# A gated delta-rule layer with a ternary feed-forward on one core: matrices and merge of the next pair placed ahead of the head scaling

## The reference, cut to what matters

```python
# x: [8, 256, 256] float32; 6 heads, DK = 32, DV = 64
q = silu(causal_conv4(x @ Wq.T)); k = silu(causal_conv4(x @ Wk.T)); v = silu(causal_conv4(x @ Wv.T))
beta = sigmoid(x @ Wb.T)
g = -exp(A_log) * softplus(x @ Wa.T + dt_bias)
q = l2norm(q) * DK ** -0.5; k = l2norm(k)
for t in range(T):                      # per batch row and head
    S = S * exp(g[t])
    S = S + beta[t] * outer(k[t], v[t] - k[t] @ S)
    o[t] = q[t] @ S
o = o * rsqrt(mean(o * o) + 1e-5) * norm_w * silu(x @ Wg.T)
h = layernorm(x + o @ Wo.T)
hq = where(h > 0.33, 0.5, where(h < -0.33, -0.5, 0))
wq = where(W > 0.2, 0.6, where(W < -0.2, -0.6, 0)) + rram_variation
return layernorm(h + hq @ wq.T)
```

## Time and profile before

| | |
|---|---|
| time, median of 3 runs | 342.59 us (339.65 to 344.24) |
| the profiled execution, its own time | 342.39 us |
| its span, and what lies around it | 340.6 us, 1.8 us |
| PE busy | 253.0 us (74%) |
| DVE busy | 260.6 us (77%) |
| ACT busy | 153.5 us (45%) |
| POOL busy | 9.2 us (3%) |
| mean DMA rate | 29 GB/s |

### The profile page before, as it was taken

How to read it: one execution, slowest core, us unless ns; L and a number is a source line. 1 busy time by engine, 2 the same in 40 slices (tenths; PEclk the granted TensorE clock), 3 DMA queues, 4 the chain that set the end, 5 groups by cost and what they waited for, 6 DMA issues and landing times.

```text
span 340.6 us, 15160 instructions
## 1 busy us (share of the span) xinstructions
PE 253.0 (74%) x6980; PEld 173.2 (51%) x6980; DVE 260.6 (77%) x648; ACT 153.5 (45%) x283; POOL 9.2 (3%) x14
## 2 busy tenths in 40 slices
PE   1969845799678977987689949988828449957561
PEld 0435412475565554756554635767607348755331
DVE  0588999774799996886999995979999951429966
ACT  1487773155664701736547405665423034235031
POOL 2110000000100000001000000010000000000000
PEclk9999987599989996999999967999987858999898
DMA  7900000000000001000000110000010002000101
GB/s 218 379 13 2 3 1 0 4 4 4 6 4 4 1 0 65 6 4 4 5 7 0 62 38 30 6 5 6 4 62 2 0 6 66 4 5 8 58 2 63
DMA packets 8032, 9.83 MB, mean 29 GB/s; under 512 B 1568, under 2 KB 7072, under 8 KB 7968
## 3 DMA queue, kind: packets, MB, share of 16 engines
q1 hardware_dynamic: 6480, 8.39, 7.3%
q10 hardware_dynamic: 1488, 0.47, 0.6%
HBM read 6.76 MB, written 2.10 MB: 26 GB/s over the span
## 4 chain that ended last, share of the span: by engine, by line
PE 54%; DVE 21%; issue 15%; ACT 7%; DMA 2%; DVEq 0%; SPq 0%; ACTq 0%
PE fr L322 15%; PE pj L335 10%; PE pj L350 5%; PE pg L322 5%; PE pc L322 4%; PE fr L425 4%; PE po L322 3%; PE pc L484 3%; DVE conv_buf L976 3%; PE po L484 2%; PE pj L514 2%; DMA xt<-x_t 2%; ACT kq L692 2%; DVE tok_buf L988 1%; DVE ss L1009 1%
## 5 line engine op out<-in xcount | busy, mean ns | idle before, releaser
L335 PE MATMUL pj<-xt,wproj 128*128 128x512 f32 x96 | 51.2, 682 | 8.9 <-DMA xt<-x_t 7.1
L976 DVE SCALAR_TENSOR_TENSOR conv_buf<-raw,wconv,conv_buf 128x512 f32<-128x512 f32 x72 | 53.4, 755 | 4.8 <-ACT conv_buf L668 3.1
L335 PEld LDWEIGHTS pj<-xt,wproj 128*128 128x128 f32 x96 | 19.4, 213 | 32.1 <-issue 25.0
L667 ACT ACTIVATE raw<-pj 128x512 f32<-128x512 f32 x24 | 14.3, 596 | 31.3 <-PE pj L335 31.3
L350 PE MATMUL pj<-xt,wproj 128*128 128x512 f32 x48 | 24.8, 659 | 4.5 <-ACT conv_buf L668 4.5
L322 PE MATMUL fr<-x_t,x 32*32 32x16 f32 x768 | 10.7, 204 | 20.7 <-issue 20.7
L322 PEld LDWEIGHTS fr<-x_t,x 32*32 32x32 f32 x768 | 10.1, 142 | 21.9 <-issue 21.9
L350 PEld LDWEIGHTS pj<-xt,wproj 128*128 128x128 f32 x48 | 10.0, 212 | 16.3 <-issue 8.4
L988 DVE STREAM_TRANSPOSE tok_buf<-kq 128x1536 f32<-128x1536 f32 x4 | 7.1, 1776 | 13.5 <-ACT kq L692 13.5
L732 ACT ACTIVATE mq<-fr 128x512 f32<-128x512 f32 x12 | 7.2, 597 | 22.1 <-PE fr L322 22.1
L322 PEld LDWEIGHTS fr<-kga,wu 32*32 32x32 f32 x768 | 11.4, 105 | 10.2 <-issue 10.2
(11 more groups left out here) (183 smaller groups left out, 569.0 us busy)
## 6 DMA issues: line engine op xcount, KB each, us to landing
xt<-x_t SPq DMA_DIRECT2D x1, 1536.0 KB, 11.9
res<-x SPq DMA_DIRECT2D x3, 512.0 KB, 4.1
out<-hid_buf SPq DMA_DIRECT2D x6, 256.0 KB, 2.1
wproj<-w_proj SPq DMA_DIRECT2D x1, 1024.0 KB, 8.0
xt<-x_t SPq DMA_DIRECT2D x1, 512.0 KB, 5.7
kq<-x SPq DMA_DIRECT2D x1, 512.0 KB, 3.9
wout<-w_out SPq DMA_DIRECT2D x1, 384.0 KB, 12.1
cst<-consts ACTq DMA_DIRECT2D x1, 305.5 KB, 11.1
```

What stands on the lines that cost most here:

```text
L335: mm = pe.matmul(pj[:, j % 2, :], wproj[:, t, j * P:(j + 1) * P], xt[:, t, k * TOK:(k + 1) * TOK], start=(t == 0), stop=(t == KT - 1))
L667: act.activation(raw[:, j, :, TAPS - 1:], bank, ACT.Copy)
L976: e = dve.scalar_tensor_tensor(out=conv[:, d, :, :], in0=raw[:, d, :, m:m + T], scalar=wconv[:, j, m:m + 1], in1=conv[:, d, :, :], op0=ALU ...
```

## The change

The order of the three lists is changed, and with it which PSUM banks some steps use.

- DVE: `head_norm` is split into `head_factors` (sum, rsqrt) and `head_scale` (scaling and transposes). `head_factors(k)` stays ahead of `chunk_matrices(k + 1)`; `head_scale(k)` and `gated(k)` stand behind `inverse_to_rows(k + 1)`, at the end of the turn. In the next turn `inverse` comes first, then two `conv_taps`, the attention sums and first norm of pair k - 1, two more `conv_taps`, `ternary`, `kq_to_tokens`, and the last two `conv_taps`.
- PE: `chunk_products` stand ahead of `exponents`. Behind the four projections of pair k + 2 come the gates of pair k (of both pairs 2 and 3 in turn 2), projections 4 and 5 of pair k + 2, then `merge(k + 1)`. `project_out(k - 1)` stands between `merge_second(k)` and `solved(k)` and writes to the banks of `pj`. `ternary_turned(k - 1)` moves behind chunk 2 of the loop, the two `feed_forward` parts behind chunks 3 and 4.
- ACT: `normalize(k - 1, 0)` moves behind `state_out(k, 0)`, `ternary_out` to chunk 3, the third `silu` ahead of the third transition's copy, the three value `silu` to chunks 4 to 6, all head squares behind the loop; the gates' SiLU and two tile copies close the turn.
- The ternary values move from `tok_buf` to `hid_buf`; the last pair's gate goes to used columns of `xt`.
- Last turn: the first half of the last heads (`end_heads(0)`) is done inside the turn behind `ternary`, the second half at its end.
- The prologue has no gates; projections 4 and 5 of pair 1 stand ahead of `merge(0)`.

```diff
--- before.py
+++ after.py
...
 gate = view(gate_buf, 0, GATE_TILES, TOK)
+gate_last = (xt[:, 0, 0:TOK], xt[:, 0, TOK:2 * TOK], xt[:, 1, 0:TOK])
...
 res = sb("res", [P, TT, HID])
-pos = view(tok_buf, 0, TT, HID, dt=BF16)
-xq = view(tok_buf, TT * HID // 2, TT, HID, dt=BF16)
+pos = view(hid_buf, 0, TT, HID, dt=BF16)
+xq = view(hid_buf, TT * HID // 2, TT, HID, dt=BF16)
...
 f_bank = (pj[:, 1, :], pj[:, 0, :])
+a_bank = (pj[:, 0, :], pj[:, 1, :])
+
+def gate_bank(k, j):
+
+    return pj[:, (j + (k == PAIRS - 1)) % 2, :]
...
             after(pe, tile_out, j - 1, k, CONV_TILES)
-        if not first(k) and j >= 4:
-            after(pe, gate_done, GATE_TILES, k - 1, GATE_TILES)
+        if k > 1 and j >= 4:
+            after(pe, gate_done, GATE_TILES, k - 2, GATE_TILES)
...
     def gates(k, j):
...
-        if j < 2:
-            if last(k):
-                after(pe, dexp_done, 1, k, 1)
-            else:
-                after(pe, tile_out, j + 3, k + 1, CONV_TILES)
+        if last(k):
+            gone = GATE_TILES * (k - 1) + j + 2
+            pe.wait_ge(gate_done, gone)
+        elif j == 2:
+            after(pe, gate_done, 1, k, GATE_TILES)
+        elif last(k + 1):
+            after(pe, dexp_done, 1, k + 1, 1)
         else:
-            after(pe, gate_done, 1, k, GATE_TILES)
+            after(pe, tile_out, j + 3, k + 2, CONV_TILES)
...
             w = CONV_TILES + j
-            mm = pe.matmul(pj[:, j % 2, :], wproj[:, t, w * P:(w + 1) * P],
+            mm = pe.matmul(gate_bank(k, j), wproj[:, t, w * P:(w + 1) * P],
...
         after(pe, tile_out, CONV_TILES, k, CONV_TILES)
-        if not first(k):
-            after(pe, gate_done, 0, k, GATE_TILES)
-            after(pe, ffn_in, 0, k - 1, 2)
+        if k > 1:
+            after(pe, ffn_in, 2, k - 2, 2)
...
             after(pe, v_tok_done, 1, k, 1)
-            if not first(k):
-                after(pe, y_in, 0, k, 2)
...
             after(pe, og_done, GATE_TILES, k, GATE_TILES)
+            if last(k + 1):
+                after(pe, gate_done, GATE_TILES, k + 1, GATE_TILES)
+            else:
+                after(pe, tile_out, CONV_TILES, k + 2, CONV_TILES)
...
             for j in range(GATE_TILES):
-                mm = pe.matmul(y_bank[part][:, (n % 2) * HID:(n % 2 + 1) * HID],
+                mm = pe.matmul(a_bank[part][:, (n % 2) * HID:(n % 2 + 1) * HID],
...
     def ternary_turned(k):
...
         after(pe, xq_done, 1, k, 1)
-        if last(k + 1):
-            after(pe, gate_done, GATE_TILES, k + 1, GATE_TILES)
-        else:
-            after(pe, tile_out, 5, k + 2, CONV_TILES)
...
                 pe.wait_ge(w_split, 3)
-            if not last(k + 1):
-                after(pe, tile_out, CONV_TILES, k + 2, CONV_TILES)
...
     def turn(k, front):
         merge_second(k)
-        if front:
-            project(k + 1, 5)
-        solved(k, 0)
-        solved(k, 1)
-        if not first(k):
-            ternary_turned(k - 1)
-        for b in range(2, 5):
+        if not first(k):
+            project_out(k - 1, 0)
+            project_out(k - 1, 1)
+        for b in range(5):
...
             transitions(k, b)
-            if not front and b < 2:
-                feed_forward(k - 1, b)
...
             heads_out(k, c)
-            if front and not first(k) and c in (2, 3):
-                feed_forward(k - 1, c - 2)
+            if not first(k) and c == 2:
+                ternary_turned(k - 1)
+            if not first(k) and c in (3, 4):
+                feed_forward(k - 1, c - 3)
         if front:
-            exponents(k + 1)
...
                 chunk_products(k + 1, g)
+            exponents(k + 1)
...
                     project(k + 2, j)
-            gates(k + 1, 0)
-            gates(k + 1, 1)
-            project_out(k, 0)
-            project_out(k, 1)
-            gates(k + 1, 2)
+            for j in range(GATE_TILES):
+                gates(k, j)
+            if last(k + 1):
+                for j in range(GATE_TILES):
+                    gates(k + 1, j)
+            else:
+                project(k + 2, 4)
+                project(k + 2, 5)
             merge(k + 1)
-            if not last(k + 1):
-                project(k + 2, 4)
...
     def decay_gate(i):
...
         project(1, j)
-    for j in range(GATE_TILES):
-        gates(0, j)
     decay_sums(1)
+    project(1, 4)
+    project(1, 5)
     merge(0)
-    project(1, 4)
...
     def gate_silu(k, j):
         after(act, gate_mm, j + 1, k, GATE_TILES)
-        if j == 0 and not first(k):
+        if j == 0 and not first(k) and not last(k):
             after(act, og_done, 0, k, GATE_TILES)
-        act.activation(gate[:, j, :], pj[:, j % 2, :], ACT.Silu).then_inc(gate_done, 1)
+        dst = gate_last[j] if last(k) else gate[:, j, :]
+        act.activation(dst, gate_bank(k, j), ACT.Silu).then_inc(gate_done, 1)
...
     def normalize(k, n):
...
             weight_part(1)
-        if front:
-            tile_out_of_psum(k + 1, 4)
-        if not first(k):
-            normalize(k - 1, 0)
-        if front:
-            tile_out_of_psum(k + 1, 5)
-        solved_out(k, 0)
-        solved_out(k, 1)
-        if not first(k):
-            ternary_out(k - 1)
-        for b in range(2, 5):
+        for b in range(5):
...
             silu(k + 1, 0)
+        if not first(k):
+            normalize(k - 1, 0)
...
         transition_out(k, 1)
-        transition_out(k, 2)
...
             silu(k + 1, 2)
+        transition_out(k, 2)
...
                 heads_out(k, c // 2)
-            if not front:
-                if c % 2:
+                if not front:
                     heads_square(k, c // 2)
-                continue
-            if c == 1:
-                silu(k + 1, 3)
-            if c == 2:
+            if front and c == 2:
                 square(k + 1)
-            if 3 <= c < 5:
-                silu(k + 1, c + 1)
-            if c >= 5:
-                heads_square(k, c - 5)
-            if c == NC - 1:
-                heads_square(k, 3)
+            if not first(k) and c == 3:
+                ternary_out(k - 1)
+            if front and c >= 4 and c < NC - 1:
+                silu(k + 1, c - 1)
         if front:
+            for n in range(NC // 2):
+                heads_square(k, n)
...
             for j in range(GATE_TILES):
-                gate_silu(k + 1, j)
+                gate_silu(k, j)
+            if last(k + 1):
+                for j in range(GATE_TILES):
+                    gate_silu(k + 1, j)
+            else:
+                tile_out_of_psum(k + 2, 4)
+                tile_out_of_psum(k + 2, 5)
...
     def soft_plus(i):
...
         tile_out_of_psum(1, j)
-    for j in range(GATE_TILES):
-        gate_silu(0, j)
     decays(1)
+    tile_out_of_psum(1, 4)
+    tile_out_of_psum(1, 5)
...
     def kq_to_tokens(k):
         after(dve, silu_done, 3, k, CONV_TILES)
-        if k > 1:
-            after(dve, xqt_mm, 0, k - 1, 1)
...
     def head_eps(k):
...
-    def head_norm(k):
+    def head_factors(k):
...
             shifts()
+
+    def head_scale(k):
...
         after(dve, y_mm, n + 1, k, 2)
-        dve.tensor_tensor(hid[:, 2 * n:2 * n + 2, :].rearrange("p n c -> p (n c)"), y_bank[n][:, :],
+        dve.tensor_tensor(hid[:, 2 * n:2 * n + 2, :].rearrange("p n c -> p (n c)"), a_bank[n],
...
     def ternary(k):
         after(dve, normed, 1, k, 1)
-        if not last(k):
-            after(dve, kg_done, 1, k + 1, 1)
...
     def end_gate(s):
...
         for j in range(GATE_TILES):
-            o_half, g_half = (a[:, j, :].rearrange("p (b s t) -> p b s t", b=2, s=2)[:, :, s, :]
-                              for a in (o_ch, gate))
+            o_half, g_half = (a.rearrange("p (b s t) -> p b s t", b=2, s=2)[:, :, s, :]
+                              for a in (o_ch[:, j, :], gate_last[j]))
...
                                      op0=ALU.mult, op1=ALU.mult).then_inc(end_gated, 1)
+
+    def end_heads(s):
+        end_head_sums(s)
+        rsqrt(head_r[s], head_v[s], t_all[:, 0:UF])
+        end_head_scale(s)
+        end_to_channels(s)
+        end_gate(s)
...
     def end_factors(bank, s):
...
     def turn(k, front):
         head_eps(k)
+        inverse(k)
         if first(k):
-            conv_taps(1, 0)
             ffn_weights(2)
-        else:
+        if front:
+            conv_taps(k + 1, 0)
+            conv_taps(k + 1, 1)
+        if not first(k):
...
             first_norm(k - 1)
-        inverse(k)
+        if front:
+            conv_taps(k + 1, 2)
+            conv_taps(k + 1, 3)
...
             ternary(k - 1)
+        if not front:
+            end_heads(0)
         if front:
-            for j in range(first(k), 5):
-                conv_taps(k + 1, j)
             kq_to_tokens(k + 1)
+            conv_taps(k + 1, 4)
...
             shifts()
+            end_heads(1)
...
         v_to_tokens(k + 1)
-        head_norm(k)
-        gated(k)
+        head_factors(k)
...
         inverse_to_rows(k + 1)
```

(8 more changed lines are left out.)

## The result

The changed kernel takes 352.07 us (median of 4 runs, 350.98 to 357.49) against 342.51 us (median of 4 runs, 339.65 to 344.24). The ratio is 1.027 with a 95% interval of 1.022 to 1.032: slower, by about 9 us. The profiled execution took 351.01 us (span 349.1).

What follows compares the result with a forecast made beforehand. It took DVE, alternating with PE on the chain, as fullest in a steady turn. Turns 0 to 3 summed as -6.9 - 4.6 - 2.4 + 7.2 = -6.7 us from 342.4; predicted 335.6, range 329 to 343.

Steps and rivals of the forecast that it cites:

- The floor and its sum: Steady turn: DVE needs 64.2 us whatever the order; the waits left on DVE are added to that.
- turn 3: Last turn: `end_heads(1)` starts at X+49.5 to 49.7 instead of X+42.5, so 7.2 us are lost.
- One wait for a gate's SiLU, which I estimate at 0.9: PE before projection 4, ahead of the merge: 0.9 us of wait, with the merge starting near X+2.4.
- X: Moment marked in each turn: the end of the second transpose in `inverse_to_rows`; X+n is n us later.
- I put 1.4: PE in the merge of a steady turn: 1.4 us of instruction wait, the second half ending at X+9.3.
- Rival 3: Slower: instruction waits in both merge halves, `project_out` and first `solved` parts at 1.2 GHz; +8 us, 350; chance 0.1.
- 68.3 us with the low clock: Steady turn: 64.2 + 1.5 + 0.7 + 1.7 + 0.2 for the feed-forward sums; 67.8 was taken.
- the 1.5 us to spare: Head squares in a steady turn: ready at X+49, DVE arriving at X+50.5, so hidden.
- `project_out` ahead of `solved`: PE behind the merge: `project_out` takes 6.9 us, so `solved` starts at X+16.2 instead of X+11.1.
- the gain of 7.1 us from the scaling: DVE: `head_scale` and `gated`, 7.1 us, leave the path ahead of the matrices and stand after X.
- Turn 0: First turn: exponentials in at 106.7, X at 121.0, 58.4 us long, 6.9 us gained.
- The reading that I had drawn: PE: filling the idle stretch before the merge leaves the clock up for `project_out`, saving 1.7 us a turn there.

Runs made afterwards that it cites:

- run 7: Changed kernel with projection 5 between the merge's halves, and on ACT `normalize(k-1, 1)` behind the gates' SiLUs: 348.62 us.
- Runs 2 and 3: 2: changed kernel, projection 5 moved between the merge's halves, 347.66 us. 3: kernel before, projection 4 moved from between them to ahead of the merge, 345.37 us.
- run 1: Changed kernel with `project_out` multiplying only one of its three head tiles (result not the reference's): 342.92 us, ratio 1.001.
- run 4: Changed kernel with both projections 4 and 5 between the two halves of the merge: 347.8 us, ratio 1.010.
- run 10: Kernel before with DVE's wait for the merge filled by three convolution tiles of the next pair, keys' work sooner, some steps later: 340.34 us, ratio 0.989.

## Why the prediction was wrong

**What held.** The floor and its sum: 64.2 us plus DVE's waits gives each steady turn within 0.2 us. The keys' transpose stood at `solved`+12.5 us in turn 1 (forecast 12.8), the squares ended at `solved`+33.8 (33), PE's wait for `ternary_out` was 1.5 to 2.1 us (1.8), `project_out` took 7.1 to 7.9 us (6.9), and turn 3 lost 7.6 (7.2). The prologue gained 0.8 where nothing was forecast.

**"One wait for a gate's SiLU, which I estimate at 0.9."** Ahead of turn 1's merge PE waited 0.24 + 0.78 us for the gates' SiLUs, ahead of turn 2's 2.20 + 0.78. ACT loads a table (1.28 us) before the SiLUs in both, and in the second it does `normalize` (2.07 us) too; both stood in no term. The merge started at X+2.8 and X+3.9 and not X+2.4. What this is worth in the time stays open: run 7 took the 2.20 away and shows no gain.

**"I put 1.4" for instruction waits in the merge.** Measured in both halves: 2.7, 4.4, 3.4 and 4.9 us in turns 0 to 3. This is the step that failed. For the first half alone (0, 2.1, 0 and 2.7) 1.4 was about the mean; the second half was put at its 2.06 us of work with no wait at all, and there the waits were 2.7, 2.3, 3.4 and 2.2 us. I had read the 2.17 us of the earlier trace rows as an accident of turn 1, while the same change took away the wide group behind which such waits were hidden. Runs 2 and 3 show what the group hid, and turn 3 of the kernel before, which has no group there, had shown it too:

```profile
274.80 1.91 PE L322 MATMUL pg<-x,p_sb 32*32 32x16 f32 x128 [0.53 <-issue]
278.80 0.29 PE L322 MATMUL pg<-x,p_sb 32*32 32x16 f32 x4 [2.10 <-issue]
```

Over the whole span the table of waits puts 47.6 us of PE's idle time down to "issue" before and 40.7 after. But 17.1 of the 47.6 stand ahead of the first matmul of a merge (5.68, 2.23, 4.51 and 4.71 us), and 1.5 of the 40.7; these end 0.8 us before X, when DVE's first transpose is done, so they are waits for DVE. Without them the instruction waits grew from 30.5 to 39.2 us.

From those in the merge comes most of DVE's waits of 4.83 and 5.37 us at L1091 where 1.5 was forecast, and 3.0 and 2.0 us of the 3.0 and 4.4 by which `solved` is late against the forecast in turns 1 and 2 (the rest of turn 2: merge start 1.5, `project_out` 1.0). Rival 3 had a wait in each half, with its break-even at `solved` = X+20; its X+22.4 was too late because it put `project_out` at 8.7 us and added 1.4 for the first parts of `solved` themselves.

**"68.3 us with the low clock".** The squares and the feed-forward sums follow `solved`. With `solved` at X+19.2 and X+20.6 the feed-forward sum came 1.70 and 2.33 us late (0.2 forecast). The squares ended at X+53.0 and X+54.7 and not at X+49, past the 1.5 us to spare, but DVE was late itself by then and did not wait for them.

**`project_out` ahead of `solved`.** Its size was right, and its place was in the sum, but run 1 shows what the sum concealed: most of it is on the path, so the gain of 7.1 us from the scaling is given back at once by PE work of the same size. The change traded DVE work for PE work on a chain on which the two alternate.

**Turn 0.** Forecast -6.9, measured -3.6. The instruction waits on PE add up to 11.7 us in this turn, 6.5 before (without the wait for DVE); `solved` came at X+8.9 and not X+7.4. The exponents ended at 108.20 and not 105.7 us, and DVE waited 2.61 us for them at L1039.

**The clock.** In the changed kernel PE ran at full clock (PEclk 1.00, that is 2.4 GHz) from 113 to 123 us, dense up to the merge, and then fell during it. The windows below are of the changed kernel: the dense stretch, the merge of turn 1 and `project_out` behind it, the same two in turn 2.

```profile
113.00:123.00 10.00, 8.98 (x21) 3.62 (x20) 8.91 (x32) 6.88 (x11) 0.00 (x0) 1.00 0.00 0
...
126.30:135.70 9.40, 4.28 (x385) 3.98 (x384) 4.69 (x10) 1.67 (x3) 0.00 (x0) 0.82 0.02 5
135.70:142.80 7.10, 7.10 (x36) 5.73 (x32) 6.11 (x9) 0.00 (x0) 0.00 (x0) 0.76 0.00 0
199.00:209.00 10.00, 5.89 (x383) 4.62 (x384) 4.94 (x10) 2.58 (x5) 0.00 (x0) 0.75 0.01 3
209.00:217.00 8.00, 8.00 (x44) 6.40 (x36) 6.10 (x9) 0.00 (x0) 0.00 (x0) 0.68 0.01 2
```

Dense work before the merge did not carry the clock through it; at a granted clock of 1.00 (run 4, turn 1, from 137.2 to 142.7 us) the same 24 matmuls took 5.45 us. The reading that I had drawn from the Trainium skill's rule ("TensorE: Matmul & The Clock Gate", section "What's actually happening"), that filling the stretch before the merge would save 1.7 us in `project_out`, did not come true here.

## What to carry to other kernels

Before a block of wide matmuls is moved away from between stretches of small ones, ask what it hides besides data waits: here its 2 to 4 us cost little, because the small matmuls would have waited for their instructions in most of that time. To see it beforehand, count instructions: in these traces, where small matmuls came to one instruction wait after another, the 256 matmuls and weight loads between took 3.3 to 5.0 us, while dense 32x32 ones of the merge are 1.9 us of work. The wait that DVE had at its meeting point with PE was better filled with work that nobody waits for (convolutions of the next pair, run 10) than with work whose move drags a piece of the other engine's chain ahead of the meeting point. And where a rival adds up waits that the trace shows in more than one turn, it deserves more than a tenth of the chance. Last, a wait that a profile puts down to "issue" can be a wait for another engine: look at what ended when it ended.
